# A selective-scan stage with its side work placed one slot sooner

## The chip, the cores and the metric

The kernel runs on one NeuronCore of a Trainium2 chip. The time is device microseconds (us) of one launch; the kernel before takes 1756.34 us, the median of three runs between 1755.08 and 1762.23 us.

## What is computed

The whole program is a four-part network on `x` of shape (4, 512, 512): a selective-scan (Mamba) layer, a mixture of experts, a cross attention and a ternary-weight feed-forward layer, each added to `x` with a tanh gate. Only the first part is touched by the change:

```python
x = jnp.einsum('bld,ed->bel', hidden_states, in_proj_w)        # in projection
xc = conv(x, conv_w, 4 taps, causal, one filter per channel)
x = silu(xc + conv_b[None, :, None])                            # u below
x_dbl = jnp.einsum('bdl,ed->bel', x, x_proj_w)
dt_low, Bm, Cm = jnp.split(x_dbl, [dt_rank, dt_rank + d_state], axis=1)
dt = jax.nn.softplus(jnp.einsum('brl,dr->bdl', dt_low, dt_proj_w) + dt_proj_b[None, :, None])
def step(state, inp):                                           # over 512 positions
    dA = jnp.exp(d[..., None] * A)
    state = state * dA + (d * u)[..., None] * b[:, None, :]
    y = jnp.einsum('bdn,bn->bd', state, c)
y = (y + D[None, :, None] * x) * silu(z)                        # z: layernorm of x
```

## The kernel before

There are 4 batches of 512 positions and 512 inner channels with 16 states each. A **slot** J is one quarter of the channels (128, index `et`) for a pair of states: two scans on VectorE (`scan(J, 0)` and `scan(J, 1)`, L447), each 128 rows by 512 positions. A batch has 32 slots, s = 0 to 31, so the stage has 128 slots, J = 32b + s. Each engine runs its own list written out slot by slot, and semaphores tie the lists together. Per slot:

- ScalarE (ACT) scales two pieces of the scan inputs (`scale_input`, L332) for a later slot group, then computes two decays (`decays(J + 3)`, L353). The decay ring has 8 buffers, so the second of these decays needs the second scan of slot J - 1.
- TensorE (PE) turns the inputs of slot J + 1 into PSUM (`turn_inputs`, L584: four 128x128 transposes for each of the two scans), and between them sums the outputs of slot J - 2 (`sums`, L597). The PSUM ring `m_d` has three banks, so the second `turn_inputs(J + 1, 1)` needs the first scan of slot J.
- VectorE (DVE) runs the two scans.
- GpSimd (POOL) multiplies the two scan results by C (L255).

Into these lists the work that prepares the next batch p = b + 1 is woven, and it shares a single PSUM bank, `m_misc`:

- **Projection and convolution, slots 0 to 5.** PE `project(p, et)` (L526) stands at the end of slot et, after `turn_inputs` and, in batches 1 and 2, after `sum_start` (L590). It needs `m_misc` free, that is, the convolution of et - 1 done. DVE `convolve(p, et)` (one L411, three L414) stands in slot et + 1. ACT `silu` (L278) of parts 0 and 1 and then the four `gates` (L287) stand in slot 3, parts 2 and 3 in slot 5, each with activation table loads. Gate t of batch b waits for the gate product of t in batch b - 1 (`gate_sum`, L455), which DVE does in slot t. In batch 0 the layernorm columns (`ln_columns`, L475 and L477) stand in slot 3 ahead of the convolution.
- **Softplus, slots 10 to 23.** PE `dt_product` (L558) stands in slots 10, 13, 16, 19, and from the second on it needs the series of the part before finished, since both use `m_misc`. ACT `logs` (L315 to L321: abs, relu, exp, ln) stands in slots 11, 14, 17, 20. Then DVE computes a series for small arguments: `series_first` (L421, L422, L424) in slots 12, 15, 18, 21 and `series_last` (L429, L431, L433) in slots 13, 16, 19, 22. POOL adds (`add_relu`, L235) in slots 14, 17, 20, 23 and multiplies by u (`times_u`, L240) one slot later.
- **Turning dt*u, slots 22 to 26.** PE `turn_dtu` (L570) in slots 22 to 25, which needs the last series, and ACT `copy_dtu` (L327) in slots 23 to 26.

PE reaches its side work in order: an instruction queued behind a waiting `project` or `dt_product` waits too, the next `turn_inputs` among them.

Of the kernel before, what the change touches and what calls it, by code (L numbers as in the profile page):

```python
# [17 lines left out]
B, L, D = 4, 512, 512  # L18
# [6 lines left out]
E4 = D // P  # L25
# [10 lines left out]
def mamba(nc, x_sb, ident, identb, tg, a, c_dram, xg_dram, zeros, s_zero):  # L36
# [13 lines left out]
    with ExitStack() as ctx:  # L50
# [92 lines left out]
        def bank(p, et):  # L143
            return first[et] if p == 0 else pm
# [70 lines left out]
        @block.gpsimd  # L215
        def _(pool):
            pool.memset(zeros[:], 0.0).then_inc(s_z0, 1)

            def scale_input(N, k):
                p, n, tb = N // PAIRS, N % PAIRS * 2 + k // TB, k % TB  # L220
                pool.tensor_scalar(dBuT[:, N % 2, tb].rearrange("p g (i c) -> p g i c", i=2)[:, :, k // TB, :],
                                   dtuT[:, p % 2, tb].rearrange("p (g c) -> p g c", g=G8),
                                   BT[:, p % 2, tb, n:n + 1], None, ALU.mult).then_inc(s_sp, 1)

            def scale_first():
                pool.wait_ge(s_dttc, E4)
                pool.wait_ge(s_btc, 1)
                for n in (6, 7):
                    scale_input(0, n)

            def add_relu(p, et):
                m = E4 * p + et
                pool.wait_ge(s_q, 6 * m + 6)
                pool.wait_ge(s_rel, m + 1)
                pool.tensor_tensor(dt[:, et], dt[:, et], ll[:, et % 2], ALU.add).then_inc(s_dt, 1)  # L235

            def times_u(p, et):
                m = E4 * p + et
                pool.wait_ge(s_dt, m + 1)
                pool.tensor_tensor(conv[:, et], dt[:, et], u[:, et], ALU.mult).then_inc(s_dtu, 1)  # L240

            for et in range(E4):
                add_relu(0, et)
                times_u(0, et)
            scale_first()
            for J in range(LAST):
                N, et, s, p = J // E4, J % E4, J % SLOTS, J // SLOTS + 1
                if p < B and s in (14, 17, 20, 23):
                    add_relu(p, (s - 14) // 3)
                if p < B and s in (15, 18, 21, 24):  # L250
                    times_u(p, (s - 15) // 3)
                if et == 0:
                    pool.wait_ge(s_c[N % RC], 32 * (N // RC + 1))
                pool.wait_ge(s_scan, 2 * J + 2)
                pool.tensor_tensor(hs[:, J % RH], hs[:, J % RH],  # L255
                                   C2[:, N % RC].unsqueeze(1).broadcast_to([P, 2, L]), ALU.mult).then_inc(s_hc, 1)
# [140 lines left out]
        def _(dve):  # L397
# [6 lines left out]
            def convolve(p, et):  # L404
                m = E4 * p + et
                z = bank(p, et)
                dve.wait_ge(s_xin, m + 1)
                if p >= 1:
                    dve.wait_ge(s_u, E4 * p)
                    dve.wait_ge(s_dtt, m - E4 + 1)  # L410
                dve.tensor_scalar(conv[:, et], z[:], conv_w[:, et, 3:4], None, ALU.mult).then_inc(s_cv, 1)  # L411
                for k in range(1, 4):
                    dve.wait_ge(s_cv, 4 * m + k)
                    dve.scalar_tensor_tensor(conv[:, et, k:L], z[:, 0:L - k], conv_w[:, et, 3 - k:4 - k],  # L414
                                             conv[:, et, k:L], ALU.mult, ALU.add).then_inc(s_cv, 1)

            def series_first(p, et):
                m, q, e = E4 * p + et, conv[:, et], bank(p, et)
                dve.wait_ge(s_l, m + 1)
                dve.wait_ge(s_u, E4 * (p + 1))  # L420
                dve.tensor_scalar(q, e[:], -0.25, None, ALU.mult).then_inc(s_q, 1)  # L421
                dve.tensor_scalar(small[:, et % 2], e[:], 1.0 / 32, None, ALU.is_lt).then_inc(s_q, 1)  # L422
                dve.wait_ge(s_q, 6 * m + 1)
                dve.scalar_tensor_tensor(q, q, 1.0 / 3, e[:], ALU.add, ALU.mult).then_inc(s_q, 1)  # L424

            def series_last(p, et):
                m, q, e = E4 * p + et, conv[:, et], bank(p, et)
                dve.wait_ge(s_q, 6 * m + 3)
                dve.scalar_tensor_tensor(q, q, -0.5, e[:], ALU.add, ALU.mult).then_inc(s_q, 1)  # L429
                dve.wait_ge(s_q, 6 * m + 4)  # L430
                dve.scalar_tensor_tensor(e[:], q, 1.0, e[:], ALU.add, ALU.mult).then_inc(s_q, 1)  # L431
                dve.wait_ge(s_q, 6 * m + 5)
                dve.copy_predicated(ll[:, et % 2], small[:, et % 2], e[:]).then_inc(s_q, 1)  # L433
# [7 lines left out]
            def scan(J, h):  # L441
                j = 2 * J + h
                dve.wait_ge(s_dA, j + 1)
                dve.wait_ge(s_dbu, j + 1)
                if J >= RH and h == 0:
                    dve.wait_ge(s_y, J - RH + 1)
                dve.tensor_tensor_scan(hs[:, J % RH, h], dA[:, j % RA], pd[j % RD][:], 0.0, ALU.mult, ALU.add)\  # L447
                    .then_inc(s_scan, 1)

            def gate_sum(b, et):  # L450
                dve.wait_ge(s_gate, TB * b + et + 1)
                dve.wait_ge(s_y, SLOTS * (b + 1) - E4 + et + 1)
                if b >= 1 and et == 0:
                    dve.wait_ge(s_t, E4 * b)
                dve.tensor_tensor(ty[:, et], py[et][:], gate[:, et], ALU.mult).then_inc(s_g, 1)  # L455

            def add(b, et):
                dve.wait_ge(s_t, E4 * b + et + 1)
                xv = x_sb[:, b * TB:(b + 1) * TB, et * P:(et + 1) * P]
                dve.scalar_tensor_tensor(xv, (first[et] if b == B - 1 else pm)[:].rearrange("p (t c) -> p t c", t=TB),  # L460
                                         tg[:, 0:1], xv, ALU.mult, ALU.add).then_inc(s_add, 1)
# [11 lines left out]
            def ln_columns():  # L473
                dve.wait_ge(s_sd, 1)
                dve.reciprocal(rstd[:], rstd[:]).then_inc(s_ln, 1)  # L475
                dve.wait_ge(s_ln, LN_RSTD)
                dve.scalar_tensor_tensor(nmr[:], mv[:, :, 0], -1.0, rstd[:], ALU.mult, ALU.mult).then_inc(s_ln, 1)  # L477
# [12 lines left out]
            for J in range(LAST):  # L490
                b, s = J // SLOTS, J % SLOTS
                p = b + 1
                scan(J, 0)
                scan(J, 1)
                if b >= 1 and s < E4:
                    gate_sum(b - 1, s)
                if b == 0 and s == 3:
                    ln_columns()
                if p < B and 1 <= s <= E4:
                    convolve(p, s - 1)  # L500
                if p < B and s in (12, 15, 18, 21):
                    series_first(p, (s - 12) // 3)
                if p < B and s in (13, 16, 19, 22):
                    series_last(p, (s - 13) // 3)
                if b >= 1 and 27 <= s < 31:
                    add(b - 1, s - 27)
            for et in range(E4):
# [1885 lines left out]
```

## Time and profile before

| | |
|---|---|
| median of three runs | 1756.34 us |
| profiled execution | 1761.8 us |
| its span | 1759.7 us |
| PE busy | 1540.0 us, 88% |
| DVE busy | 1177.1 us, 67% |
| ACT busy | 1006.3 us, 57% |
| POOL busy | 518.1 us, 29% |
| scan stage | about 59.5 to 507 us of the span |
| batch 1, slots 0 to 31 | 116.00 us |

Busy times are means over four stages with different limits; what matters here is the stretch of the scan stage. In it a start time is in microseconds from the span's start, and the number in square brackets is how long the engine stood idle before the row and which work released it. Two back-to-back instructions start about 0.1 us closer together than their durations say, since the end of one overlaps the start of the next. The granted TensorE clock is given as a share of full speed: 1.00 is 2.4 GHz and 0.50 is 1.2 GHz.

### The profile page before, as it was taken

To read this page: it belongs to the slowest core of one execution; us is meant where nothing else is said; L and a number is where in the kernel's file an instruction comes from. 1 tells how busy PE (TensorE), PEld (TensorE's weight loads), DVE (VectorE), ACT (ScalarE), POOL (GpSimd) and SP (SyncE) were. 2 spreads that over 40 slices of the span, in tenths; PEclk is the share of its full clock that TensorE was granted. 3 is DMA by queue.
4 is the path that set the end of the run, shared out by engine and by line. 5 is a ranking of instruction groups with operands and counts; after the bars stand their busy time and mean duration, and the time that the engine had idled before them with its cause. 6 is when DMAs were issued, how large, how long until landed. Compare 5 with 4: busy or idle time off the path is not lost. (4 is left out here: it accounts for less than half of the span.)

```text
span 1759.7 us, 22630 instructions
## 1 busy us (share of the span) xinstructions
PE 1540.0 (88%) x6580; PEld 669.6 (38%) x6581; DVE 1177.1 (67%) x1726; ACT 1006.3 (57%) x1551; POOL 518.1 (29%) x314
## 2 busy tenths in 40 slices
PE   5688878879857999999998789589999999898997
PEld 1334334334432444444443333123333333244543
DVE  7688988989885222222225749568888888369875
ACT  3798988979933001111113332357777777678775
POOL 1478678678860710000005446340000000000000
PEclk7698988979978999999999889689999999999999
DMA  5101102002472545458526453543332333020000
GB/s 176 42 31 46 51 19 67 18 13 72 137 255 94 191 62 190 150 177 274 177 85 200 130 126 112 199 79 79 74 84 71 83 74 81 29 96 1 31 30 36
DMA packets 105352, 173.47 MB, mean 99 GB/s; under 512 B 18323, under 2 KB 52499, under 8 KB 104259
## 3 DMA queue, kind: packets, MB, share of 16 engines
q1 hardware_dynamic: 83750, 124.62, 24.4%
q0 software_dynamic: 6624, 23.14, 4.4%
q10 hardware_dynamic: 14912, 24.89, 4.2%
q8 instruction: 34, 0.56, 0.1%
q14 instruction: 32, 0.26, 0.1%
HBM read 109.29 MB, written 54.92 MB: 93 GB/s over the span
## 5 line engine op out<-in xcount | busy, mean ns | idle before, releaser
L1582 DVE TENSOR_REDUCE a_mx<-a_s 128x2 f32<-128x1024 f32 x256 | 301.1, 1218 | 58.5 <-PE a_s L1704 57.0
L255 POOL TENSOR_TENSOR m_hs<-m_hs,m_C 128x1024 f32<-128x1024 f32 x128 | 301.3, 2367 | 117.0 <-DVE m_hs L447 116.4
L447 DVE TENSOR_TENSOR_SCAN m_hs<-m_dA,m_d 128x512 f32<-128x512 f32 x256 | 296.9, 1205 | 53.6 <-PE m_d L584 32.9
L859 ACT ACTIVATE e_sg<-e_gu 128x256 f32<-128x256 f32 x63 | 24.2, 383 | 312.8 <-PE e_gu L1091 312.8
L584 PE MATMUL m_d<-ident_sb,m_dBuT 128*128 128x128 f32 x1024 | 169.4, 300 | 27.4 <-ACT m_dBuT L332 14.4
L584 PEld LDWEIGHTS m_d<-ident_sb,m_dBuT 128*128 128x128 f32 x1024 | 122.4, 151 | 176.3 <-DVE m_hs L447 104.9
L1724 PE MATMUL a_t<-ring_sb 99*128 99x512 bf16 x512 | 181.1, 393 | 7.2 <-ACT early_sb L1486 3.8
L1486 ACT ACTIVATE a_pr<-a_t 128x512 f32<-128x512 f32 x256 | 142.3, 596 | 63.1 <-PE a_t L1724 61.9
L353 ACT ACTIVATE m_dA<-m_dt,m_negA 128x512 f32<-128x512 f32 x256 | 170.4, 712 | 7.7 <-DVE m_hs L447 7.6
L1704 PE MATMUL a_s<-ring_sb 96*128 96x512 bf16 x512 | 152.8, 390 | 24.3 <-DMA ring_sb<-qk_dram 14.1
L1486 ACT ACTIVATE early_sb<-a_t 128x512 f32<-128x512 f32 x256 | 142.2, 596 | 51.6 <-PE a_t L1724 50.6
L1091 PE MATMUL e_gu<-e_w,e_xgT 128*128 x376 | 169.3, 593 | 0.9 <-issue 0.9
L332 ACT ACTIVATE m_dBuT<-m_dtuT,m_BT 128x512 f32<-128x512 f32 x251 | 166.2, 712 | 0.1
L597 PE MATMUL m_y<-m_hs,m_fold 128*64 128x512 f32 x512 | 152.0, 675 | 2.9 <-POOL m_hs L255 2.9
L1012 DVE TENSOR_TENSOR e_hm<-e_sg,e_gu 128x256 f32<-128x256 f32 x63 | 26.5, 421 | 190.5 <-ACT e_sg L859 190.4
L1724 PEld LDWEIGHTS a_t<-ring_sb 99*128 99x128 bf16 x512 | 42.3, 98 | 187.2 <-ACT early_sb L1486 83.2
L1934 POOL MEMSET f_ones<- 128x128 f32 x1 | 0.2, 205 | 375.2 <-POOLq L1207 375.2
L1091 PEld LDWEIGHTS e_gu<-e_w,e_xgT 128*128 128x128 f32 x376 | 67.8, 190 | 68.8 <-issue 68.8
L1107 PE MATMUL e_y<-e_w,e_hT 128*128 x188 | 88.6, 593 | 1.0 <-DVE e_hT L1018 1.0
L1406 POOL MEMSET w_sb<- 128x384 f32 x1 | 0.8, 773 | 277.4 <-POOLq L2304 277.4
L1704 PEld LDWEIGHTS a_s<-ring_sb 96*128 96x128 bf16 x512 | 48.7, 100 | 78.0 <-DMA ring_sb<-qk_dram 14.6
L1042 DVE COPY e_yo<-e_y 128x512 f32<-128x512 f32 x46 | 31.8, 692 | 58.8 <-PE e_y L1107 58.8
(308 smaller groups left out, 2386.3 us busy)
## 6 DMA issues: line engine op xcount, KB each, us to landing
ring_sb<-qk_dram SPq DMA_DIRECT2D x384, 64.0 KB, 2.8
e_w<-in_ex_gu SPq DMA_DIRECT2D x16, 1024.0 KB, 6.7
xg_dram<-zeros_sb SPq DMA_DIRECT2D x2, 6016.0 KB, 28.5
e_xg<-xg_dram ACTq DMA_DIRECT2D x47, 256.0 KB, 2.7
yg_dram<-e_yo ACTq DMA_DIRECT2D x47, 256.0 KB, 2.0
m_C<-c_dram SPq DMA_DIRECT2D x64, 128.0 KB, 2.9
m_dt<-m_dt SPq DMA_DIRECT2D x64, 128.0 KB, 2.4
e_w<-in_ex_dn SPq DMA_DIRECT2D x16, 512.0 KB, 8.3
```

Source lines behind the costliest of these rows:

```text
L255: pool.tensor_tensor(hs[:, J % RH], hs[:, J % RH], C2[:, N % RC].unsqueeze(1).broadcast_to([P, 2, L]), ALU.mult).then_inc(s_hc, 1)
L332: act.activation(dBuT[:, N % 2, tb].rearrange("p g (i c) -> p g i c", i=2)[:, :, k // TB, :], dtuT[:, p % 2, tb].rearrange("p (g c) -> p g ...
L353: act.activation(dA[:, j % RA], dt2[:, g], ACT.Exp, scale=negA[:, g * PAIRS + q:g * PAIRS + q + 1]).then_inc(s_dA, 1)
L447: dve.tensor_tensor_scan(hs[:, J % RH, h], dA[:, j % RA], pd[j % RD][:], 0.0, ALU.mult, ALU.add)\
L584: last = pe.transpose(pd[j % RD][:, t * P:(t + 1) * P], dBuT[:, N % 2, t, g], ident[:])
L597: last = pe.matmul(py[et][64 * h:64 * h + 64, :], fold[:], hs[:, J % RH, h], start=False, stop=True, skip_group_check=True, tile_position= ...
L1091: last = pe.matmul(pgu[par][:], lhs(k), rhs(k), start=(k == 0), stop=(k == KD - 1))
L1107: last = pe.matmul(pyo[par][:], hT[:, par, k], rhs(k), start=(k == 0), stop=(k == KF - 1))
L1486: act.activation(pr[r % 2][:, h, kt], pst[:, kt % 2], ACT.Exp).then_inc(s_e, 1)
L1582: dve.tensor_reduce(mx[:, r % 2, h * TB + 2 * c:h * TB + 2 * c + 2], psc[c][:], AX.X, ALU.max)\
L1704: last = pe.matmul(psc[c][:, q], qs[0:KR, ring_at, h, qt * P:(qt + 1) * P], ks[0:KR, ring_at, h], start=True, stop=True)
L1724: pe.matmul(pst[:, kt % 2], ks[0:KM, ring_at, h, kt * P:(kt + 1) * P], qs[0:KM, ring_at, h], start=True, stop=True).then_inc(s_t, 1)
```

## The change

Only the slot numbers of DVE's and POOL's side work change. Each convolution, each `series_first` and `series_last`, each `add_relu` and `times_u` is one slot sooner. PE's, ACT's and SP's lists stay as they are, as do all buffers and semaphores.

```diff
 @block.gpsimd
+                if p < B and s in (13, 16, 19, 22):
+                    add_relu(p, (s - 13) // 3)
                 if p < B and s in (14, 17, 20, 23):
-                    add_relu(p, (s - 14) // 3)
-                if p < B and s in (15, 18, 21, 24):
-                    times_u(p, (s - 15) // 3)
+                    times_u(p, (s - 14) // 3)
 @block.vector
-                if p < B and 1 <= s <= E4:
-                    convolve(p, s - 1)
+                if p < B and s < E4:
+                    convolve(p, s)
+                if p < B and s in (11, 14, 17, 20):
+                    series_first(p, (s - 11) // 3)
                 if p < B and s in (12, 15, 18, 21):
-                    series_first(p, (s - 12) // 3)
-                if p < B and s in (13, 16, 19, 22):
-                    series_last(p, (s - 13) // 3)
+                    series_last(p, (s - 12) // 3)
```

On DVE, at the start of batch 1 (slots 0 to 2), the list is as follows; L455 is the gate product, L447 x2 the two scans of a slot, and the four rows L411 and L414 one convolution.

```order
-L447 SCALAR_TENSOR_TENSOR m_hs<-m_dA,m_d 128x512 x20
-L455 TENSOR_TENSOR m_ty<-m_y,m_gate 128x512
-L447 SCALAR_TENSOR_TENSOR m_hs<-m_dA,m_d 128x512 x2
-L455 TENSOR_TENSOR m_ty<-m_y,m_gate 128x512
-L411 TENSOR_SCALAR m_conv<-m_misc,m_conv_w 128x512
+L447 SCALAR_TENSOR_TENSOR m_hs<-m_dA,m_d 128x512 x22
+L455 TENSOR_TENSOR m_ty<-m_y,m_gate 128x512
+L411 TENSOR_SCALAR m_conv<-m_misc,m_conv_w 128x512
+L414 SCALAR_TENSOR_TENSOR m_conv<-m_misc,m_conv_w,m_conv 128x511
+L414 SCALAR_TENSOR_TENSOR m_conv<-m_misc,m_conv_w,m_conv 128x510
+L414 SCALAR_TENSOR_TENSOR m_conv<-m_misc,m_conv_w,m_conv 128x509
```

The last series piece of batch 0 now leaves 22 scans and not 20 before the first gate product, and the first convolution stands straight behind that gate product instead of behind the next two scans and the next gate product.

On DVE in slots 4 to 15 of batch 0 before, the series of the first part stands behind 16 scans, counted from the last convolution; its two halves are the rows L421 to L424 and L429 to L433.

```order
L414 SCALAR_TENSOR_TENSOR m_conv<-m_misc,m_conv_w,m_conv 128x509
L447 SCALAR_TENSOR_TENSOR m_hs<-m_dA,m_d 128x512 x16
L421 TENSOR_SCALAR m_conv<-m_misc 128x512
L422 TENSOR_SCALAR m_small<-m_misc 128x512
L424 SCALAR_TENSOR_TENSOR m_conv<-m_conv,m_misc 128x512
L447 SCALAR_TENSOR_TENSOR m_hs<-m_dA,m_d 128x512 x2
L429 SCALAR_TENSOR_TENSOR m_conv<-m_conv,m_misc 128x512
L431 SCALAR_TENSOR_TENSOR m_misc<-m_conv,m_misc 128x512
L433 COPY_PREDICATED m_ll<-m_small,m_misc 128x512
L447 SCALAR_TENSOR_TENSOR m_hs<-m_dA,m_d 128x512 x4
```

These rows read the same in the changed list, since the convolutions ahead of them moved by the same one slot; what moved is the slot they stand in. The 16 scans are those of slots 5 to 12 before and of slots 4 to 11 now.

On POOL around slot 13 of batch 0 (L255 is the product with C, one for each slot, L235 the addition):

```order
-L255 TENSOR_TENSOR m_hs<-m_hs,m_C 128x1024 x14
+L255 TENSOR_TENSOR m_hs<-m_hs,m_C 128x1024 x13
 L235 TENSOR_TENSOR m_dt<-m_dt,m_ll 128x512
 L255 TENSOR_TENSOR m_hs<-m_hs,m_C 128x1024
```

The first addition moved ahead of the product of slot 13.

## Rows read from the trace of the kernel before

**Rows 1.** Waits, 59 to 507 us: who waited for whom: total us, times, longest us.

```profile
DVE m_hs L447 <- PE m_d L584: 32.9, 35, 3.0
...
PE m_misc L558 <- DVE m_ll L433: 22.5, 9, 2.5
ACT m_ee L315 <- PE m_misc L558: 21.9, 9, 3.5
...
PE m_misc L526 <- DVE m_conv L414: 12.9, 8, 3.7
```

**Rows 2.** Windows, batch 1: busy PE, PEld, DVE, ACT, POOL; clock, DMA share, GB/s.

```profile
183.00:299.00 116.00, 98.78 (x453) 47.67 (x452) 102.11 (x111) 100.86 (x161) 82.87 (x39) 0.90 0.16 42
```

**Rows 3.** Timeline of DVE, batch 1, slots 0 to 2: start, us, work, [idle before].

```profile
183.00 0.67 DVE L455 TENSOR_TENSOR m_ty<-m_y,m_gate 128x512 f32<-128x512 f32 x1
...
186.40 0.74 DVE L411 TENSOR_SCALAR m_conv<-m_misc,m_conv_w 128x512 f32<-128x512 f32 x1
...
189.41 2.32 DVE L447 TENSOR_TENSOR_SCAN m_hs<-m_dA,m_d 128x512 f32<-128x512 f32 x2
```

**Rows 4.** Timeline of PE, batch 1, slots 0 and 1.

```profile
183.62 1.88 PE L526 MATMUL m_misc<-m_ctxT,m_w_in 128*128 128x512 f32 x4
...
185.87 1.08 PE L597 MATMUL m_y<-m_hs,m_fold 128*64 128x512 f32 x4
186.88 0.66 PE L584 MATMUL m_d<-ident_sb,m_dBuT 128*128 128x128 f32 x4
187.38 1.02 PE L590 MATMUL m_y<-m_u,m_diagD 128*128 128x512 f32 x2
```

**Rows 5.** Timeline of ACT, batch 1, slots 3 to 6.

```profile
192.51 1.28 ACT L278 ACT_TABLE_LOAD   x1
...
200.31 1.33 ACT L332 ACTIVATE m_dBuT<-m_dtuT,m_BT 128x512 f32<-128x512 f32 x2
...
209.28 1.33 ACT L332 ACTIVATE m_dBuT<-m_dtuT,m_BT 128x512 f32<-128x512 f32 x2
```

**Rows 6.** The same three engines in batch 0, slots 0 to 6.

```profile
65.04 1.88 PE L526 MATMUL m_misc<-m_ctxT,m_w_in 128*128 128x512 f32 x4
...
83.60 3.78 PE L526 MATMUL m_misc<-m_ctxT,m_w_in 128*128 128x512 f32 x4 [3.69 <-DVE m_conv L414]
...
80.57 2.93 ACT L287 ACTIVATE m_gate<-x_sb,m_nmr,m_rstd 128x512 f32<-128x512 f32 x4 [3.20 <-DVE m_nmr L477]
...
93.78 1.34 ACT L332 ACTIVATE m_dBuT<-m_dtuT,m_BT 128x512 f32<-128x512 f32 x2
...
78.25 2.28 DVE L477 SCALAR_TENSOR_TENSOR m_nmr<-m_mv,m_rstd 128x16 f32<-128x16 f32 x1
```

**Rows 7.** Timeline of DVE, batch 1, slots 12 to 21.

```profile
228.00 0.67 DVE L421 TENSOR_SCALAR m_conv<-m_misc 128x512 f32<-128x512 f32 x1
...
229.77 2.33 DVE L447 TENSOR_TENSOR_SCAN m_hs<-m_dA,m_d 128x512 f32<-128x512 f32 x2
232.01 0.67 DVE L429 SCALAR_TENSOR_TENSOR m_conv<-m_conv,m_misc 128x512 f32<-128x512 f32 x1
...
252.77 1.22 DVE L447 TENSOR_TENSOR_SCAN m_hs<-m_dA,m_d 128x512 f32<-128x512 f32 x1 [1.75 <-PE m_d L584]
...
267.45 0.67 DVE L421 TENSOR_SCALAR m_conv<-m_misc 128x512 f32<-128x512 f32 x1
```

**Rows 8.** Timeline of PE, batch 1, slots 13 and 16.

```profile
234.23 1.12 PE L558 MATMUL m_misc<-m_xdbl,m_w_dt 16*128 16x512 f32 x2 [2.54 <-DVE m_ll L433]
...
246.60 2.07 PE L558 MATMUL m_misc<-m_xdbl,m_w_dt 16*128 16x512 f32 x2 [2.53 <-DVE m_ll L433]
```

**Rows 9.** Timeline of ACT, batch 1, slots 11 and 26.

```profile
225.08 0.67 ACT L315 ACTIVATE m_ee<-m_misc,m_dt_b 128x512 f32<-128x512 f32 x1
...
227.05 0.60 ACT L321 ACTIVATE m_ll<-m_misc 128x512 f32<-128x512 f32 x1
...
285.44 0.58 ACT L327 ACTIVATE m_dtuT<-m_misc 128x512 f32<-128x512 f32 x1
```

## The prediction, as it was recorded

> **What bounds the kernel now.** The change touches only the scan stage, so I read that stretch of the trace and leave the rest of the span as it is. First the waits of the stretch [rows 1]: the scans waited 32.9 us for PE's turned inputs, while PE's `dt_product` waited 22.5 us for the end of a series, ACT's `logs` 21.9 us for that product, and PE's `project` 12.9 us for a convolution. Then the windows [rows 2]: in batch 1 no engine is full (PE 98.78, DVE 102.11, ACT 100.86 of 116.00 us, the first a busy time that a slow clock swells). So what sets the pace is chains between engines, and the timelines show two kinds.
>
> In slots 1 to 4 DVE is full. From a gate product to the next scans it runs without a gap: the convolution begins at 186.40 and takes 3.01 us to the scans at 189.41 [rows 3]. The projection that it needs (1.88 us, [rows 4]) ran beside the scans, which is what the slot between the two is for.
>
> In slots 13 to 22 a serial loop rules. PE stands at `dt_product` (idle 2.53 us at 246.60) until the series ends, takes 2.07 us for it, and only then turns the inputs for the scan that DVE waits 1.75 us for at 252.77 [rows 7, 8]. From one `series_first` (228.00) to the last of the four (267.45) is 39.45 us, 13.15 us a part [rows 7].
>
> **Durations, from rows.** A slot's two scans 2.24 us (229.77 to 232.01), the first of them 1.13; `series_first` 1.77 (228.00 to 229.77); `series_last` 2.16 (232.01 to the release of PE at 234.2) [rows 7, 8]. Convolution 3.01, gate product 0.58, projection 1.88, one `turn_inputs` 0.6, `sum_start` 1.0, `sums` 1.05 [rows 3, 4]. `logs` 2.57 (225.08 to 227.65) [rows 9]. Two ACT pieces 1.22, so a plain ACT slot 2.45 [rows 5]. Four gates 2.93, so one 0.7; a table load 1.28; two silus 1.3 [rows 5, 6]. Handovers between engines are taken as 0.05.
>
> **Part 1, the convolutions: work that needs PE's projection in the same slot.** PE's list is unchanged: in slot s it ends with `turn_inputs` (which needs the first scan of slot s), `sum_start`, `project(p, s)`. A convolution in slot s now waits for all of this, and the scans queued behind it on DVE wait too. Batch 1, in the times of this trace:
> - Slot 0: scans end at 183.1, gate product 183.6, projection done at 185.5 [rows 3, 4]. The convolution runs 185.55 to 188.55 (1.9 us of stall).
> - Slot 1: first scan done 189.7, both 190.8, gate product 191.4. PE: `turn_inputs` to 190.3, `sum_start` to 191.3, projection to 193.15. Convolution 193.2 to 196.2.
> - This is a loop of first scan 1.13 + 0.6 + 1.0 + 1.88 + convolution 3.01 = 7.6 us, where DVE alone has 2.24 + 0.58 + 3.01 = 5.83. Slot 2 ends at 203.8, slot 3 at 211.4.
> - ACT: the decays of slot 3 need the scans of slot 2 (198.4), end 199.1; load 200.4, silus 201.7; the fourth gate now waits for DVE's gate product of slot 3, which stands behind the convolution of slot 2 (203.8 + 2.24 + 0.58 = 206.6). Gates end 207.3, load 208.6, slot 4 211.05. Slot 5: two pieces 212.3, decays wait for the scans of slot 4 (213.65), end 214.3; load, silus, load (3.9) 218.1. Before, ACT began slot 6 at 209.28 [rows 5]: **+8.8 us**. From here ACT is back to back to slot 11, so nothing takes this back. Batch 2 repeats batch 1: +8.8.
> - Batch 0 has no gate products and no `sum_start`, but the scans of slot 1 already wait: projection done 66.9 [rows 6], convolution 69.9, scans 72.2. Then first scan 71.1 + 0.6 + 1.88 gives 73.5, convolution 76.6, scans 78.8; next convolution 83.2, scans of slot 3 85.4; the layernorm columns (2.5 us to the end of the 2.28 at 78.25, [rows 6]) 87.9, last convolution 90.9. Gates from 87.95 to 90.9 (they followed the columns at 80.57 too), load 92.2, slots 4 and 5 97.1, load, silus, load 101.1. Before 93.78 [rows 6]: **+7.3 us**.
> Together +24.9 us.
>
> **Part 2, the series: the loop opens.** `dt_product` no longer meets an unfinished series: with `series_last` in slot 12, the product of slot 13 stands behind `turn_inputs`, which needs the first scan of slot 13 anyway. What is late next is `logs`, since DVE asks for it in its own slot. Batch 1, counted from an unmoved `logs(0)` that ends at 227.65 [rows 9]:
> - `series_first` 227.7 to 229.5 (before 228.00, but after the scans of slot 12, which now come behind it: a loss of one slot's scans at the start). Scans 12 end 231.7, `series_last` 233.9, scans 13 236.1.
> - The loop from there: second decay of slot 14 (0.65), `logs` 2.57, `series_first` 1.77, scans 2.24, `series_last` 2.16, scans 2.24: 11.7 us against 13.15. Twice: scans 19 end 259.5.
> - `logs(3)` done 262.7, `series_first` 264.5, scans 21 266.8, `series_last` 268.95, scans 22 271.2, decay 271.85, `copy_dtu(0)` 272.4, then ACT: slot 24 275.35, slot 25 278.3, and the last copy begins at 280.75. Before 285.44 [rows 9]: **-4.7 us**.
> I take the same for each batch: -14.1 us.
>
> POOL's pieces are no term: POOL is busy 82.87 of 116.00 us [rows 2] and the series that they wait for comes a slot sooner too. SP's list does not move; its dt copies start with `add_relu`, sooner. Nothing on DVE is added or removed.
>
> **Part 3, PE's clock.** Both parts assume PE at full speed. At 246.60, after 2.53 us idle, the product took 2.07 us against 1.12 at 234.23, and the projection at 83.60, after 3.69 us idle, took 3.78 against 1.88 [rows 4, 6, 8]: half speed, 1.2 for 2.4 GHz. In the new convolution loop PE has done `turn_inputs` and `sums` 1.6 us after a projection and then stands idle until the first scan is done, 3.01 + 1.13 - 1.65 = 2.5 us. If it is then at half speed, its 3.5 us on the loop become 7.0. Bounds for the nine loops: 0 and 9 x 3.5 = 31 us. An idle of 1 us was harmless, one of 2.5 costs in some cases; I take about 1 us a loop, +9. In the series part the first product of each batch stands behind a PE wait of 3.4 us (227.2 to 230.6, the stalled scans of slot 12) and is likely slow: its 0.95 and 0.45 of `turn_inputs`, 1.4 us, are not hidden; the other six have a wait of 2 us well ahead of them, and I take 0.3 each. Bounds 0 and 9 x 1.4 = 12.6; taken 4.2 + 1.8 = 6.
>
> The Trainium skill, TensorE: Matmul & The Clock Gate, section "A second HAM failure mode: psum-queue depth-cycling", says that short idles between groups of matmuls, one for each pass over the PSUM banks, are enough to make the clock swing between its two levels. The row at 246.60 agrees. By this rule in full the sum would stand near the upper bounds; with none of it, at +10.8 us.
>
> **Sum.** +24.9 - 14.1 + 9 + 6 = +25.8 us, of which parts 1 and 2 are +10.8. The profiled execution was 1761.8 us, so it would be about 1788; from the median of 1756.34 us the same term gives **1782 us**.
>
> **Rivals.**
> - *PE keeps its clock* (+10.8, 1767 us). For it: half of the slow stretches before may have come from the `dt_product` wait, which goes. Against: the new idles of 2.5 us in the convolution loop.
> - *Faster: the series loop is the only one that counts* (1742 us). The convolution's waits would be lost in slack that ACT has in slots 1 to 5, so only -14.1 us is left. It decides if ACT's slot 6 comes no later than 26.2 us after the last scan of the batch before (209.28 - 183.08). For it: ACT waits there for DVE already. Against: ACT is loaded with 7 us of gates and loads in slot 3, all behind the scans of slot 2.
> - *The two terms cancel* (1756 us): convolution loops shorter than worked out, such as 5.83 + 0.9, which would halve part 1 to about +13.
> - *PE at half speed in most loops* (24.9 - 14.1 + 25 + 10 = +46, 1802 us). For it: the waits come with every part.
>
> **Chances.** Forecast (1782) 0.58; clock kept (1767) 0.21; cancel 0.07; faster 0.07; half speed throughout 0.07. The range takes in the first two and reaches to the edge of the last: 1763 to 1801 us. A difference under 0.5% (8.8 us) can't be told from none here; the case of the kept clock lies just above it, so a part of it counts as same. Faster 0.07, same 0.10, slower 0.83.
>
> **What would show it.** In the trace of the changed kernel: PE's waits for a series at `dt_product` gone from its list, ACT waiting for it under 1 us; convolutions waiting about 1 to 2 us each for `project`, 12 times; ACT's slot 6 of batch 1 about 35 us or more after the last scan of batch 0; `series_first` waiting about 1 us for `logs` in slots 14, 17, 20 and 3 us in slot 11; parts 11.7 us apart, or up to 13 with a slow product. Wrong would be: scans of slots 0 to 4 still 5.83 us apart, or ACT's fourth gate not waiting for a gate product in batch 1.

## The result and the profile after

The changed kernel takes 1787.6 us in the median of four runs (1780.85 to 1789.83), the kernel before 1756.83 us: a ratio of 1.017, 95% interval 1.0147 to 1.0192. The change makes the kernel about 31 us slower. The profiled execution was the fastest of the four, 1780.85 us with a span of 1778.9 us. That of before (1761.8 us) was near the slow end of its own, so the two traces lie only 19 us apart.

The stretch before the scans is as it was: PE is busy 28.63 us in it, before 28.61. What changed lies in the scan stage. Columns as in [rows 2]; the rows are these two stretches, for the changed kernel.

```profile
0.00:59.50 59.50, 28.63 (x58) 12.07 (x60) 40.86 (x81) 25.06 (x41) 14.29 (x15) 0.67 0.54 157
59.50:531.00 471.50, 374.57 (x1768) 178.98 (x1766) 390.43 (x405) 387.43 (x609) 329.75 (x152) 0.92 0.19 58
```

The layer's next part begins with a normalisation on DVE. Its first instruction stands at 512.6 us before and at 535.6 us after, so the scan stage grew by 23.0 us in these two executions; the rest of the program was 3.8 us shorter. Of the two rows below the first is of the kernel before, the second of the changed one; they give line, engine, operation, shortest/median/longest ns of one, and the first and last start.

```profile
L932 DVE BATCH_NORM_STATS2 e_stats<-x_sb x16: 676/681/695, 512.6 to 521.5; 128x6 f32<-128x512 f32 x16
```

```profile
L932 DVE BATCH_NORM_STATS2 e_stats<-x_sb x16: 677/682/694, 535.6 to 544.5; 128x6 f32<-128x512 f32 x16
```

The waits of the stage after, against [rows 1]:

```profile
PE m_d L584 <- DVE m_hs L447: 71.6, 49, 3.9
ACT m_dA L353 <- DVE m_hs L447: 51.2, 40, 5.9
...
DVE m_conv L411 <- PE m_misc L526: 28.4, 12, 5.2
...
DVE m_conv L421 <- ACT m_ll L321: 19.8, 12, 2.8
...
DVE m_hs L447 <- PE m_d L584: 14.1, 21, 1.8
...
ACT m_gate L287 <- DVE m_ty L455: 7.0, 2, 4.3
...
ACT m_ee L315 <- PE m_misc L558: 1.3, 1, 1.3
```

PE's waits for the series at `dt_product` are gone from the list, ACT waits for that product 1.3 us instead of 21.9, and the scans wait for PE 14.1 us instead of 32.9. In their place all twelve convolutions wait for their projection, 28.4 us, and `series_first` waits for `logs` twelve times, 19.8 us. What is lost on DVE is found again on ACT: its decays wait 51.2 us for scans, before 7.6.

DVE in batch 1, slots 0 to 2, after, against [rows 3]:

```profile
192.53 0.67 DVE L455 TENSOR_TENSOR m_ty<-m_y,m_gate 128x512 f32<-128x512 f32 x1
195.08 0.75 DVE L411 TENSOR_SCALAR m_conv<-m_misc,m_conv_w 128x512 f32<-128x512 f32 x1 [1.88 <-PE m_misc L526]
...
198.10 2.32 DVE L447 TENSOR_TENSOR_SCAN m_hs<-m_dA,m_d 128x512 f32<-128x512 f32 x2
200.34 0.67 DVE L455 TENSOR_TENSOR m_ty<-m_y,m_gate 128x512 f32<-128x512 f32 x1
202.64 0.75 DVE L411 TENSOR_SCALAR m_conv<-m_misc,m_conv_w 128x512 f32<-128x512 f32 x1 [1.63 <-PE m_misc L526]
...
210.20 0.75 DVE L411 TENSOR_SCALAR m_conv<-m_misc,m_conv_w 128x512 f32<-128x512 f32 x1 [1.63 <-PE m_misc L526]
...
219.45 0.75 DVE L411 TENSOR_SCALAR m_conv<-m_misc,m_conv_w 128x512 f32<-128x512 f32 x1 [3.33 <-PE m_misc L526]
```

The first stall is 1.88 us and the loop from convolution to convolution 7.56 us twice (195.08, 202.64, 210.20); the third is 9.25 us. PE shows why:

```profile
206.93 0.66 PE L584 MATMUL m_d<-ident_sb,m_dBuT 128*128 128x128 f32 x4 [2.88 <-DVE m_hs L447]
207.42 1.02 PE L590 MATMUL m_y<-m_u,m_diagD 128*128 128x512 f32 x2
208.28 1.88 PE L526 MATMUL m_misc<-m_ctxT,m_w_in 128*128 128x512 f32 x4
...
214.49 0.66 PE L584 MATMUL m_d<-ident_sb,m_dBuT 128*128 128x128 f32 x4 [2.88 <-DVE m_hs L447]
214.98 1.66 PE L590 MATMUL m_y<-m_u,m_diagD 128*128 128x512 f32 x2
216.43 2.98 PE L526 MATMUL m_misc<-m_ctxT,m_w_in 128*128 128x512 f32 x4
```

Both groups follow an idle of 2.88 us. One ran at full speed; in the other the clock fell within the `sum_start`, and the projection took 2.98 us. ACT in slots 3 to 6 of the same batch, against [rows 5]:

```profile
208.76 1.28 ACT L278 ACT_TABLE_LOAD   x1
...
211.29 2.21 ACT L287 ACTIVATE m_gate<-x_sb,m_nmr,m_rstd 128x512 f32<-128x512 f32 x3
216.16 0.81 ACT L287 ACTIVATE m_gate<-x_sb,m_nmr,m_rstd 128x512 f32<-128x512 f32 x1 [2.66 <-DVE m_ty L455]
...
229.51 1.33 ACT L332 ACTIVATE m_dBuT<-m_dtuT,m_BT 128x512 f32<-128x512 f32 x2
```

The fourth gate waits 2.66 us for the gate product that stands behind a stalled convolution. Slot 6 begins 229.51 - 192.53 = 37.0 us after the batch's first gate product, before 209.28 - 183.00 = 26.3. The series of batch 1 on DVE, against [rows 7]:

```profile
247.91 0.69 DVE L421 TENSOR_SCALAR m_conv<-m_misc 128x512 f32<-128x512 f32 x1 [2.79 <-ACT m_ll L321]
...
261.05 0.69 DVE L421 TENSOR_SCALAR m_conv<-m_misc 128x512 f32<-128x512 f32 x1 [2.50 <-ACT m_ll L321]
...
272.92 0.69 DVE L421 TENSOR_SCALAR m_conv<-m_misc 128x512 f32<-128x512 f32 x1 [1.24 <-ACT m_ll L321]
...
284.65 0.69 DVE L421 TENSOR_SCALAR m_conv<-m_misc 128x512 f32<-128x512 f32 x1 [1.09 <-ACT m_ll L321]
```

The parts are 13.1, 11.9 and 11.7 us apart, before 13.15 in the mean. The first is long because its product stood at half speed:

```profile
256.32 2.07 PE L558 MATMUL m_misc<-m_xdbl,m_w_dt 16*128 16x512 f32 x2
```

To split the 23.0 us I cut each batch at the last `logs` instruction of slot 11 (L321), from the first gate product of the batch (L455) to it, and from it to the next batch's first gate product. The first piece holds the convolutions, the second the series.

| | gate product to `logs(0)`, before | after | `logs(0)` to gate product, before | after |
|---|---|---|---|---|
| batch 0 | 111.55 (from the span's start) | 123.71 | 71.45 | 68.82 |
| batch 1 | 44.05 | 54.75 | 74.66 | 71.46 |
| batch 2 | 44.05 | 55.53 | 75.47 | 69.98 |
| sum of differences | | +34.3 | | -11.3 |

### The profile page after: what moved, and what is told of

Same layout as the page of the kernel before. It is cut to its first block and busy times, and to the rows that moved or that the text cites. A ratio compares the mean times of both kernels' runs of the same rounds, so it can differ in the third digit from the quotient of the medians.

```text
span 1778.9 us, 22630 instructions
## 1 busy us (share of the span) xinstructions
PE 1532.3 (86%) x6580; PEld 664.2 (37%) x6581; DVE 1176.1 (66%) x1726; ACT 1008.8 (57%) x1551; POOL 516.8 (29%) x314
## 5 line engine op out<-in xcount | busy, mean ns | idle before, releaser
L255 POOL TENSOR_TENSOR m_hs<-m_hs,m_C 128x1024 f32<-128x1024 f32 x128 | 300.8, 2370 | 141.5 <-DVE m_hs L447 141.4
L447 DVE TENSOR_TENSOR_SCAN m_hs<-m_dA,m_d 128x512 f32<-128x512 f32 x256 | 293.4, 1200 | 31.8 <-ACT m_dA L353 17.1
L584 PEld LDWEIGHTS m_d<-ident_sb,m_dBuT 128*128 128x128 f32 x1024 | 118.8, 149 | 245.7 <-DVE m_hs L447 169.6
L353 ACT ACTIVATE m_dA<-m_dt,m_negA 128x512 f32<-128x512 f32 x256 | 172.0, 713 | 51.8 <-DVE m_hs L447 51.2
```

Source lines behind the costliest of these rows:

```text
L255: pool.tensor_tensor(hs[:, J % RH], hs[:, J % RH], C2[:, N % RC].unsqueeze(1).broadcast_to([P, 2, L]), ALU.mult).then_inc(s_hc, 1)
L353: act.activation(dA[:, j % RA], dt2[:, g], ACT.Exp, scale=negA[:, g * PAIRS + q:g * PAIRS + q + 1]).then_inc(s_dA, 1)
L584: last = pe.transpose(pd[j % RD][:, t * P:(t + 1) * P], dBuT[:, N % 2, t, g], ident[:])
```

## Experiments

All ratios are to the kernel before, timed beside the experiment. Beside e5 to e8 it took 1792.45 us, about 2% more than beside the others (1757 to 1760 us). In the traces of e5 to e8 the stretch between the scan stage and the cross attention is 27 to 32 us longer than in that of the kernel before, while the scans began at the same time. So only the ratios of e5 to e8 are compared, not their times.

**e1: the convolutions alone.**

```diff
-                if p < B and 1 <= s <= E4:
-                    convolve(p, s - 1)
+                if p < B and s < E4:
+                    convolve(p, s)
```

> Only the convolutions move one slot sooner; series and GpSimd pieces stay. Theory (the convolution waits for a projection of the same slot, then ScalarE is late): every convolution waits 1.3 to 5 us for the projection, the stage grows by the 34 us read from the two traces up to logs, so about 1757 + 34 = 1791 us, a ratio of 1.019. Rival (the convolutions are neutral, the 2.8 us waits of series_first for logs do the harm): 1757 us within 5. Second rival (the two parts make each other worse): under half of it, below 1775 us.

Measured: 1792.0 us against 1759.25, ratio 1.018 (1.0144 to 1.0215). The eleven traced convolution waits come to 32.2 us, and PE's wait for the series at `dt_product` stands as before, 22.2 us:

```profile
DVE m_conv L411 <- PE m_misc L526: 32.2, 11, 6.6
...
PE m_misc L558 <- DVE m_ll L433: 22.2, 9, 2.5
```

The convolutions carry the whole loss. The rival that they are neutral is out, and so is the one that they cost under half of it alone.

**e2: the series and GpSimd's pieces alone** (the other half of the diff).

> Only the series and GpSimd's dt pieces move one slot sooner; the convolutions stay. Theory: PE's waits of 2.5 us at dt_product go, series_first waits 2.8 us for logs in slot 11 and about 1.1 us in the others, parts 11.7 to 13 us apart; faster by the 11 us read from the traces, about 1746 us, ratio 0.994. Rival (series_first in the slot of logs does the harm): slower than 1760 us.

Measured: 1746.72 us against 1759.25, ratio 0.9937 (0.9921 to 0.9953). This half is a gain. In batch 1 the four `series_first` stand at 224.85, 236.59, 248.33 and 260.06, 11.7 us apart each time; the loop had been worked out at 11.7. The rows (DVE, e2):

```profile
224.85 0.69 DVE L421 TENSOR_SCALAR m_conv<-m_misc 128x512 f32<-128x512 f32 x1 [2.79 <-ACT m_ll L321]
...
236.59 0.69 DVE L421 TENSOR_SCALAR m_conv<-m_misc 128x512 f32<-128x512 f32 x1 [1.09 <-ACT m_ll L321]
```

The waits for `logs` are real, and still the cheaper ones.

Multiplied, the ratios of e1 and e2 give 1.012. The whole change gave 1.017, and 1.0145 when it was timed again (e11). The intervals do not settle whether the two halves also cost a few microseconds by being together; that stays open.

**e7: VectorE's series alone, GpSimd's pieces where they were.**

> Only VectorE's two series halves move one slot sooner; convolutions and GpSimd's dt pieces stay where they were. Theory (GpSimd's pieces are on no path): as with the whole series part moved, 1747 us within 3. Rival (dt and dt*u have to be ready sooner too, turn_dtu would wait for times_u): 1750 to 1756 us.

Measured: ratio 0.9956 (0.9933 to 0.9979), beside 0.9937 (0.9921 to 0.9953) for e2. The intervals overlap; no share of GpSimd's part can be told from none.

**e3, e10 and e11: how much of the loss is PE's clock in the convolution loop.** The changed kernel with one addition on PE:

```diff
                 if J + 1 < LAST:
+                    if p < B and 1 <= s <= 3:
+                        for _ in range(4):
+                            turn_again(J + 1)   # turn_inputs(J + 1, 0) without its signal
                     turn_inputs(J + 1, 0)
```

> The changed kernel, with PE kept at work in slots 1 to 3 of the first three batches: the first turn_inputs of each of these slots is done four extra times into the same bank (16 extra 128x128 transposes, about 2 us) before it counts. No wait is taken away. Theory (about 9 us of the loss is the half clock after idles of 2.9 us in the convolution loop): projections at 1.88 us and no longer 3.0 to 3.6, loops 7.56 us each, about 9 us faster than the changed kernel, 1779 us. Rival (the clock costs nothing there, only the waits do): within 3 us of the changed kernel, 1787 us, or slower by the extra work.

Measured: 1779.84 us, ratio 1.0117 (1.0085 to 1.0148). All twelve projections now take 1.88 us, and PE's idle ahead of the turned inputs is down to 1.13 us in eight of the nine loops and 2.14 us in the ninth (batch 0, slot 1). PE, e3, batch 1:

```profile
202.72 1.91 PE L594 MATMUL m_d<-ident_sb,m_dBuT 128*128 128x128 f32 x16
...
207.21 0.66 PE L584 MATMUL m_d<-ident_sb,m_dBuT 128*128 128x128 f32 x4 [1.13 <-DVE m_hs L447]
207.70 1.02 PE L599 MATMUL m_y<-m_u,m_diagD 128*128 128x512 f32 x2
208.56 1.88 PE L526 MATMUL m_misc<-m_ctxT,m_w_in 128*128 128x512 f32 x4
```

Beside each other on one chip:

> The changed kernel with PE kept at work in slots 1 to 3 again, beside the unwarmed changed kernel of the same call (the two comparisons with it so far came from different calls). Theory: 9 us faster than the changed kernel. Rival: within 3 us of it.

> The changed kernel as it is, beside e10 on the same chip: ratio to before 1.017 as recorded, 9 us above e10 by the theory that the half clock in the convolution loop costs that much, within 3 us of it by the rival.

Measured: e10 1776.28 us, ratio 1.0104 (1.0074 to 1.0134); e11, the changed kernel again, 1783.6 us, ratio 1.0145 (1.011 to 1.0179). The difference is 7.3 us here, and 0.5%, 9 us, between e3 and the first timing of the changed kernel. The intervals of the two ratios overlap, but both carry the scatter of the kernel before; of the two kernels themselves, the slowest execution of e10 (1777.48 us) is faster than the fastest of e11 (1781.5 us). So the gain is real, and its size is 7 to 9 us.

The clock was not held everywhere in e10. In batch 0 an idle of 2.14 us, which e3 passed at full speed, was followed by a slow projection (PE, e10); the other eleven took 1.88 us:

```profile
71.53 0.65 PE L584 MATMUL m_d<-ident_sb,m_dBuT 128*128 128x128 f32 x4 [2.14 <-DVE m_hs L447]
72.02 3.13 PE L526 MATMUL m_misc<-m_ctxT,m_w_in 128*128 128x512 f32 x4
```

**e5: the projection at the head of its PE slot,** so that it runs beside the scans, the rest as changed.

```diff
+                if p < B and s < E4:
+                    project(p, s)
                 if J + 1 < LAST:
                     turn_inputs(J + 1, 0)
...
-                    if s < E4:
-                        project(p, s)
```

> The changed kernel, but PE's projection stands at the head of its slot instead of at its end, so that it runs beside the scans of that slot. Convolutions still stand one slot sooner than before. Theory (the convolution part costs time only because the projection stands behind turn_inputs, which waits for the scans of the same slot): convolution loops back at 5.83 us, about 2 us a batch left because ScalarE's slot 3 still finds the scans of slot 2 behind an earlier convolution; with the series gain about 1752 us, ratio 0.997. Rival (a convolution in its projection's slot is bad in any order, because it delays the scans that the decays need): the gain against the changed kernel is under 15 us, above 1772 us.

Measured: ratio 1.005 (1.0032 to 1.0069). It lies between the theory (0.997) and the rival: the gain against the changed kernel is 17 to 21 us. The loops are as forecast, 5.84 us in batch 1 with no wait at a convolution (DVE, e5):

```profile
190.43 0.74 DVE L411 TENSOR_SCALAR m_conv<-m_misc,m_conv_w 128x512 f32<-128x512 f32 x1
...
196.27 0.74 DVE L411 TENSOR_SCALAR m_conv<-m_misc,m_conv_w 128x512 f32<-128x512 f32 x1
```

But the convolution part did not come back to its old length. Measured as in the table above, from the span's start in batch 0 and from the batch's first gate product in the others, `logs(0)` ends 9.2 us later than before in batch 0, 3.0 in batch 1 and 4.6 in batch 2, 17 of the 34 us. So the order on PE was half the cause; the other half stays with the projection moved. For batches 1 and 2 I had allowed 2 us for ACT's decays and fourth gate, which find the scans behind an earlier convolution. It is 3.0, and in batch 2 the copy of the projected input (L296) waits 1.6 us longer as well. Batch 0 I had not worked out: there projections at half speed (3.33 and 3.04 us, after idles of 2.33 and 1.98 us) stand ahead of the turned inputs.

**e4: both halves of the series in slots 12, 15, 18, 21,** convolutions as before. GpSimd's pieces are one slot sooner too, as in the changed kernel; that part of the edit is not shown below.

```diff
+                if p < B and s in (12, 15, 18, 21):
                     series_first(p, (s - 12) // 3)
-                if p < B and s in (13, 16, 19, 22):
-                    series_last(p, (s - 13) // 3)
+                if p < B and s in (12, 15, 18, 21):
+                    series_last(p, (s - 12) // 3)
```

> Convolutions as before; series_first stays in slots 12, 15, 18, 21, and series_last moves into the same slots right behind it; GpSimd's dt pieces one slot sooner. Theory (the gain comes from the series being finished before dt_product asks; series_first sooner than slot 12 only adds a wait for logs): no wait at dt_product and none for logs, parts near DVE's own 10.65 us, about 5 us a batch better than the series moved whole, 1730 us. Rival (series_first has to be sooner too for the gain): no better than 1746 us.

Measured: 1752.15 us, ratio 0.9971 (0.9959 to 0.9982). A miss by 22 us, and worse than e2. No wait at `dt_product` and none for `logs`, as said; but PE stands idle 2.4 to 3.0 us behind the longer block, and part of what follows is at half speed (PE, e4):

```profile
234.42 0.65 PE L584 MATMUL m_d<-ident_sb,m_dBuT 128*128 128x128 f32 x4 [3.00 <-DVE m_hs L447]
...
246.14 0.66 PE L584 MATMUL m_d<-ident_sb,m_dBuT 128*128 128x128 f32 x4 [2.41 <-DVE m_hs L447]
246.72 1.97 PE L558 MATMUL m_misc<-m_xdbl,m_w_dt 16*128 16x512 f32 x2
248.62 1.11 PE L584 MATMUL m_d<-ident_sb,m_dBuT 128*128 128x128 f32 x4
249.66 1.98 PE L597 MATMUL m_y<-m_hs,m_fold 128*64 128x512 f32 x4
```

**e6: e4 with PE kept at work** (the four extra transposes in slots 13, 16, 19, 22).

> The kernel with both series halves in slots 12, 15, 18, 21, with PE kept at work: in slots 13, 16, 19, 22 the first turn_inputs is done four extra times (16 extra transposes) ahead of its own. Theory (it came out at 1752 and not at 1730 us because PE, idle 2.4 to 3.0 us behind the block of two halves, does dt_product and the sums behind it at half clock): parts near 10.8 us instead of 11.7 to 13.0, about 10 us faster, 1742 us. Rival (PE's serial path behind the block is too long at full clock too, or the longer block holds the product on GpSimd up): no better than 1750 us.

Measured: ratio 0.9875 (0.9828 to 0.9922), against 0.9971 for e4: 1% or some 17 us less, where 10 was forecast, for some 23 us of PE work that computes nothing new (12 groups of 1.91 us). In batch 1 parts 2 and 3 are 10.66 and 11.1 us, the first still 11.9. The rival is out. It has the lowest ratio of the study, but its interval takes in that of e9 below.

**e8: e2 with PE kept at work** (slots 12, 15, 18, 21).

> The series and GpSimd's pieces one slot sooner, convolutions as before, with PE kept at work: in slots 12, 15, 18, 21 the first turn_inputs is done four extra times ahead of its own. Theory (the product of slot 13 is slow because PE stood idle behind series_first's wait for logs): that product at 1.1 us, its logs no longer 1.3 us late, up to 4 us faster than without, 1743 us. Rival (no half clock on the path, or the extra work delays the turned inputs): 1747 us or more.

Measured: ratio 0.9918 (0.9887 to 0.9948), against 0.9937 (0.9921 to 0.9953) for e2. Inconclusive: the forecast of 0.2% is smaller than the intervals. The trace of e2 had little to give back there, since all its twelve products took 1.12 us.

**e9: the kernel before, nothing moved, PE kept at work** while it would wait for the series.

```diff
                 if J + 1 < LAST:
+                    if p < B and s in (13, 16, 19, 22):
+                        for _ in range(4):
+                            turn_again(J + 1)   # turn_inputs(J + 1, 1) without its signal
                     turn_inputs(J + 1, 1)
```

> The kernel before with nothing moved, and PE kept at work in slots 13, 16, 19, 22: the second turn_inputs is done four extra times (16 extra transposes, about 2 us) while PE would stand idle for the series. Question: how much of the series loop's 13.1 us a part is the wait and how much is the half clock behind it. Theory (the half clock is about half of it: dt_product 2.07 to 1.12, sums 1.98 to 1.08, two turned inputs 1.05 to 0.6 each, together 2.7 us on the loop in most of the nine parts): parts 10.9 to 12 us, 15 us faster than before, ratio 0.991. Rival (the wait of PE for the series sets the loop and the clock is hidden): ratio above 0.997.

Measured: 1741.49 us against 1759.71, ratio 0.9899 (0.9869 to 0.9929). More than the moved series brings without it. In batch 1 `series_first` stands at 223.28, 234.05, 245.03 and 256.43: parts of 10.8, 11.0 and 11.4 us, with the series and the product in their old slots. Over the nine parts of the three batches the mean is 11.4 us, before 13.15; two of them are still 12.6 and 13.0. From 224 to 262 us the granted clock is 1.00 (columns as in [rows 2]), before 0.83 in the same stretch. All twelve products take 1.12 us, where six of twelve took 2.07 before, and the wait ahead of them is filled (PE, e9):

```profile
224.00:262.00 38.00, 31.63 (x191) 18.14 (x189) 36.60 (x43) 34.73 (x58) 31.84 (x17) 1.00 0.07 22
```

```profile
238.15 1.97 PE L592 MATMUL m_d<-ident_sb,m_dBuT 128*128 128x128 f32 x16
239.96 0.60 PE L584 MATMUL m_d<-ident_sb,m_dBuT 128*128 128x128 f32 x4
240.49 1.12 PE L558 MATMUL m_misc<-m_xdbl,m_w_dt 16*128 16x512 f32 x2
```

So the loss in the old series loop was less the wait than the half clock that the wait brought about. DVE's own work in a part is 10.65 us (three slots of scans at 2.24, `series_first` 1.77, `series_last` 2.16). Of the 2.5 us above that, 1.75 went with the clock.

The end of the scan stage in the traces, that is, the start of the first L932 (L944 and L942 where lines were added), one execution each, as the difference to the kernel before. It leaves out the slower stretch of e5 to e8:

| kernel | us |
|---|---|
| the changed kernel; again (e11) | +23.0; +27.5 |
| e1 convolutions alone | +35.5 |
| e3; e10, changed kernel with PE kept at work | +18.3; +16.8 |
| e5 projection first | +5.5 |
| e7 VectorE's series alone | -9.0 |
| e4 both halves in slots 12, 15, 18, 21 | -9.2 |
| e8 series with PE kept at work | -11.8 |
| e2 series alone | -15.1 |
| e9 kernel before with PE kept at work | -20.4 |
| e6 e4 with PE kept at work | -20.9 |

## Why the prediction was right

**The direction and the size.** Forecast 1782 us (1763 to 1801), measured 1787.6. The case that it named likeliest, convolutions waiting in their projection's slot and PE at half speed in some loops, is what the traces show. The rival with the faster result is out by e1, the one in which the terms cancel by e1 and e2 together. The one in which PE keeps its clock is out by the slow projections and by what e10 gave back, and half speed throughout by the four loops of nine at full speed.

**Part 1, the convolutions.** The mechanism came as forecast, step by step in batch 1: stall in slot 0 forecast 1.9, measured 1.88 us; loop 7.6, measured 7.56; the fourth gate waited for its gate product as said; ACT's slot 6 later by 8.8 plus clock, measured 10.7. Against the 1 to 2 us forecast the convolutions waited 1.1 to 3.3 us, longest where the projection was slow, and 5.2 us at the first of batch 0. With the clock, forecast 33.9 us; the cut of the two traces gives 34.3, e1 alone 1.8%, about 33 us.

That the sum met so closely is in part luck. Cut the same way, e3 and e10, with PE kept at work, are 28.4 and 28.1 us longer than before in the first piece, where 24.9 had been worked out for full clock. Batches 1 and 2 are right (9.0 and 8.4, forecast 8.8 each). The shortfall is in batch 0 (11.0 and 10.7, forecast 7.3). There ACT's copy of the projected input (L296) waits 1.89 us for its product (L537) even when that runs at full speed (e10), 3.11 in the result's trace and 0.38 before, a wait that no step had.

**Part 2, the series.** Loop forecast 11.7, measured 11.72 to 11.74 in e2. Start: `series_first` waited 2.79 us for `logs` in slot 11, forecast 3. The same gain was taken for each batch, 4.7 us and 14.1 together. The second pieces of e2, with every part at 11.7 us, are 2.6, 4.7 and 5.6 us shorter than before, 12.9 together: batch 0 has less to gain.

**Part 3, the clock.** For the convolutions forecast 9 us: 34.3 - 28.2 = 6.1 in the result's trace, where five of nine projections in the loops took 2.0 to 3.6 us instead of 1.88. In the trace of e11, the same kernel, it is 37.4 - 28.2 = 9.2. For the series forecast 6: 12.9 - 11.3 = 1.6 in the result's trace, and 12.9 - 9.9 = 3.0 in e11's. This term was too large in both. The product that opens each batch's loop, taken as slow in every batch, was slow in one of three, and in two of three in e11.

| term | forecast | result's trace | e11's trace |
|---|---|---|---|
| convolutions at full clock | +24.9 | +28.2 | +28.2 |
| series at full clock | -14.1 | -12.9 | -12.9 |
| clock, convolutions | +9 | +6.1 | +9.2 |
| clock, series | +6 | +1.6 | +3.0 |
| sum | +25.8 | +23.0 | +27.5 |

The two terms at full clock are taken from e3, e10 and e2 in both columns, so the clock terms are what is left, good to 1 or 2 us. The sum at full clock was worked out as 10.8 and is about 15; the clock was taken as 15 and is 8 to 12. The two errors offset each other.

The median is 5.6 us above the forecast. The profiled execution was the fastest. That of e11 took 1785.23 us, 4.4 more, and its scan stage is 4.5 us longer, 3.1 of it in the convolutions' pieces and 1.4 in the series', with the slow stretches in other slots. So how often the clock falls accounts for the difference between these two executions of one kernel. That it also accounts for the other executions is likely, but no trace of them shows it.

**The skill's rule.** The Trainium skill, TensorE: Matmul & The Clock Gate, section "A second HAM failure mode: psum-queue depth-cycling", was weighed as an upper bound. The traces agree that short idles suffice, 2.88 us here. Not each of them does it: after the same 2.88 us PE ran at full speed in one loop and at half in the next. So the sum lay well below the upper bounds.

## What to carry to other kernels

Before moving a consumer sooner, find where its producer stands in the producer's own list: a consumer in the producer's slot waits for everything queued ahead of the producer there, and everything behind the consumer waits too. Test the parts of a combined change apart, since here a gain of 0.6% was hidden in a loss of 1.8%. And where PE waits a few microseconds inside a serial loop between engines, price the slower clock after the wait as well as the wait, and where the work behind the wait is traced at half speed, try to fill the wait before reordering anything.

## What the runs showed of the hardware

- Sixteen repeated 128x128 transposes in PE's idle time (about 2 us, twelve times) made an unchanged kernel 1.0% faster (e9, 0.9869 to 0.9929): the clock over the series loop rose to 1.00, where dt_product had shown 2.07 us against 1.12.
- An idle of 2.88 us was followed by full speed in one loop and by half speed in the next, in the same batch. After an idle of 1.13 us (e3, eight loops) full speed followed each time. After 2.14 us it was full speed in e3 and not in e10, the same kernel (projection 1.88 and 3.13 us), and in e5 an idle of 1.98 us was followed by a projection of 3.04 us.
- The kernel before took 1792.45 us beside e5 to e8 and 1757 to 1760 us beside the others, on other chips. In the traces of e5 to e8 the extra 27 to 32 us lie behind the scan stage. Kernels that were timed apart have to be compared by ratios.
